# Perceiver layer on one core: the low halves of heads 8 to 15's keys are made in the second pass over the context, not in the first

## The chip, the cores and the metric

The kernel runs on one core of one Trainium2 chip. The metric is the device time of one execution in microseconds (us). Before the change it is 483.58 us, the median of 3 runs (482.57 to 485.65).

## What is computed

A perceiver layer in float32. 128 query rows of width 256 attend with 16 heads of 16 columns to a context of 12544 rows; then the 128 rows attend to each other; then a feed-forward part whose weights and activations are rounded to a few bits. The part that the change touches is the first attention:

```python
qh = (layernorm(x) @ Wq.T + bq).reshape(128, 16, 16)
kh = (ctx @ Wk.T + bk).reshape(12544, 16, 16)
vh = (ctx @ Wv.T + bv).reshape(12544, 16, 16)
scores = einsum('qhd,khd->hqk', qh, kh) / 4
scores = where(mask, -1e7, scores)
x = x + einsum('hqk,khd->qhd', softmax(scores), vh)
```

## The kernel before

**Float32 on TensorE (PE) in parts.** PE multiplies a rounded type, f32r, in one go. A float32 number is therefore split into a high part (the number rounded to f32r) and a low part (what is left). The keys are needed in both parts.

**Two passes over the context.** The context is cut into 14 blocks (NB) of 7 tiles of 128 rows, 896 keys (BK) each. The first pass finds for every query and head a maximum of the scores; the second forms the scores again, subtracts that maximum, takes exp and adds up the values. What passes from one to the other goes through DRAM.

**First pass, a block.** It has 16 slots, of which the eight even ones hold work: by `PROJECTIONS`, four are a quarter of the keys (m = 0 holds heads 0 to 7, m = 1 heads 8 to 15; n is the half of the 896 keys) and four are values of one or two tiles. For a quarter, PE does six matmuls into `ps_k` (L888), ScalarE (ACT) adds the bias and writes the rounded keys `k_hi` (L472), and VectorE (DVE) writes what is left, `k_lo` (L657). PE may not write `ps_k` again before `lo_ready` tells that DVE has read it. Values: PE L897, ACT L478. After each slot PE also forms scores of one group of heads with the bfloat16 upper halves of `k_hi` (L931). Half of these DVE reduces to a maximum (L691); ACT copies the other half as bfloat16 (L488) and DVE takes it into a running maximum (L696). Every 8 groups DVE folds the block's maxima (L702). At slot 2j the scores belong to group j + 4 of the block before (j < 4) or to group j - 4 of this block.

**The context's own split.** ACT rounds the next block's context in four pieces (L442), and GpSimd (POOL) subtracts (L379). A piece of POOL's waits for DVE's running maxima:

```python
pool.wait_ge(run_taken, (s - 2) * NG + LAG + 2 * n)
```

so the last piece (n = 3) for the next block waits for group 1 of the present one, whose scores come at slot 10. PE's next block begins with `pe.wait_ge(ctx_split, (s + 1) * PIECES)`.

**Between the passes.** PE forms the last four groups' scores; DVE folds all running maxima (L727 to L731) while PE keeps its clock up with 23 matmuls on zeros (L942); PE turns the maxima into rows (L1016), and ACT (L548) and DVE (L737) write these into `q_stack`.

**Second pass.** `k_stack` has two buffers. Of four neighbouring rows of partitions, one holds ones (it meets the row of maxima), two hold `k_hi` and one holds `k_lo`, each by a DMA of its own (SyncE, L314: six for a block, 448 KB each). PE multiplies (L1045), ACT takes exp (L559), PE adds up the values (L1058). A block has 8 units of 6 and 8 pairs of heads. The keys of block b are loaded once block b - 2 is scored, since they take its buffer. PE's code is a loop of two blocks, gone round six times, and two blocks written out behind it (L1095). DVE has only the feed-forward weights to round here (L743 to L753).

Of the kernel before, what the change touches and what calls it, by code (L numbers as in the profile page):

```python
# [4 lines left out]
H = 16  # L5
HD = 16
D = H * HD
Q = 128
# [5 lines left out]
T = 7  # L14
# [18 lines left out]
SLOTS_P = 4  # L33

# [24 lines left out]
def perceiver_layer(nc: bass.Bass, x_d, ctx_d, maskn_d, maskt_d, wqn_d, wqr_d, bqn_d, bqr_d, wk_d, bk_d, wv_d, bv_d,  # L59
# [5 lines left out]
    k_hi_d = nc.dram_tensor("k_hi_scratch", [NB, DC, P, BK], f32, kind="Internal").ap()  # L65
# [3 lines left out]
    with ExitStack() as stack_of_contexts:  # L69
# [19 lines left out]
        ctx_bufs = (ctx_t, sb("ctx_b", [P, DC * BK])[:, :])  # L89
        k_hi = sb("k_hi", [P, 2, DC, BK], f32r)  # L90
        k_upper = k_hi[:, :, :, :].bitcast(bf16).rearrange("p b m (k h) -> p b m k h", h=2)[:, :, :, :, 1]
        k_lo = sb("k_lo", [P, DC, BK], f32r)
        k_stack = sb("k_stack", [P, 2, PR, BK], f32r)

        ctx_parts = k_stack[:, 1, :, :].rearrange("p (b c l) k -> p b c l k", b=2, c=2)
# [43 lines left out]
        magic = sb("magic", [P, 3])  # L139
        self_max = sb("self_max", [P, H], bf16)  # L140
# [27 lines left out]
        stack_in = [sem(f"stack_in{i}") for i in range(2)]  # L168
# [9 lines left out]
        hi_ready, lo_ready = sem("hi_ready"), sem("lo_ready")  # L178
        max_scored, max_taken = sem("max_scored"), sem("max_taken")
# [26 lines left out]
        s_probs_t = middle[:, H * Q:2 * H * Q].rearrange("p (j n q) -> p j n q", j=4, n=4)  # L206
        w_blocks = w_raw.rearrange("p (n b) -> p n b", b=BLOCK)
# [43 lines left out]

        def scored_in(slot):
            u = slot // 2
            return (1, u + LAG) if u < LAG else (0, u - LAG)
# [4 lines left out]
        def _(sp):  # L259
# [31 lines left out]
            def store_keys(s, par, m):  # L291
                sp.wait_ge(hi_ready, (s * DC + m + 1) * 2)
                sp.dma_start(k_hi_d[s, m], k_hi[:, par, m, :].bitcast(f32)).then_inc(hi_stored[par][m], 16)
                sp.wait_ge(lo_ready, (s * DC + m + 1) * 2)
                sp.dma_start(k_lo_d[s, m], k_lo[:, m, :].bitcast(f32)).then_inc(lo_stored[m], 16)
# [5 lines left out]
            with sp.Fori(1, NB // 2) as i:  # L301
                for par in range(2):
                    s = i * 2 - 2 + par
                    load(s + 2, par)
                    store_keys(s, par, 0)
                    store_keys(s, par, 1)
                    store_values(s, par)

            def load_keys(b, par):

                for m in range(DC):
                    for slot in range(1, STRIDE):
                        src = (k_lo_d if slot == 2 else k_hi_d)[b, m]
                        sp.dma_start(k_stack[slot::STRIDE, par, m * PR // 2:(m + 1) * PR // 2, :].bitcast(f32),  # L314
                                     src.rearrange("(p r) k -> r p k", r=2 * HD)).then_inc(stack_in[par], 16)

            def load_values(b, par):
                sp.dma_start(v_in[:, par * T * H * VW:(par + 1) * T * H * VW], v_d[b]).then_inc(v_back[par], 16)
# [7 lines left out]
            load_keys(0, 0)  # L326
# [7 lines left out]
            load_values(0, 0)  # L334
            wait_keys_stored(1)
            sp.wait_ge(consts_set, 9)
            load_keys(1, 1)
            sp.wait_ge(v_stored[1], 16)
            load_values(1, 1)
            for m in range(DC):  # L340
                for par in range(2):
                    sp.wait_ge(hi_stored[par][m], 16 * NB // 2)
                sp.wait_ge(lo_stored[m], 16 * NB)
            for par in range(2):
                sp.wait_ge(v_stored[par], 16 * NB // 2)

            sp.wait_ge(lo_ready, NB * DC * 2)
# [4 lines left out]
            with sp.Fori(1, NB // 2) as i:  # L352
                for par in range(2):
# [945 lines left out]
```

## Time and profile before

| | before |
|---|---|
| median of 3 runs | 483.58 us |
| the profiled execution: device time, span | 485.21 us, 483.50 us |
| mean granted clock of TensorE | 0.979 of full |
| busy: PE, ACT, DVE, POOL | 455.1, 384.4, 275.6, 99.6 us |
| first pass, until DVE's last running maximum | to 228.7 us |
| second pass | from 235.3 to 436 us |
| second attention and feed-forward | to 483.5 us |

The span runs from the first to the last instruction. Busy times are sums over the span, and the two passes have different limits, so they are read by stretch. The granted clock is the share of full speed that TensorE was given: it has two levels, 2.4 GHz (1.00) and 1.2 GHz (0.50).

### The profile page before, as it was taken

How to read it: one execution, taken by the hardware profiler on the slowest of the kernel's cores; microseconds unless marked ns; L12 is line 12 of the kernel's file. 1: busy time of each engine (PE TensorE's matmuls, PEld its weight loads, DVE VectorE, ACT ScalarE, POOL GpSimd, SP SyncE). 2: the span in 40 equal slices, each digit the busy share in tenths (PEclk: the TensorE clock that was granted, in tenths of full speed). 3: DMA queues.
4: the chain of work that ended last, by engine and by line, in shares of the span. 5: the costliest groups of instructions: out<-in, count | busy, mean ns of one | idle time of the engine just before them, and what ended most of it. 6: DMA issues, size and time to landing. Idle time of an engine off the chain costs nothing.

```text
span 483.5 us, 15996 instructions
## 1 busy us (share of the span) xinstructions
PE 455.1 (94%) x6464; PEld 357.4 (74%) x6464; DVE 275.6 (57%) x406; ACT 384.4 (80%) x436; POOL 99.6 (21%) x101
## 2 busy tenths in 40 slices
PE   8799999999999999996899999999999999999896
PEld 4666667666676666672588999999999999985463
DVE  5579999999999999999479400000000000004566
ACT  7678888888888888875378999999999999993423
POOL 1598532343334333305000000000000000000000
PEclk9989999999999999997789999999999999999999
DMA  8986667866668766958918877777888777500000
GB/s 263 357 335 219 262 228 292 327 241 241 256 245 327 283 238 260 379 227 315 414 57 327 326 246 263 285 269 275 301 327 309 268 263 265 209 3 2 1 1 14
DMA packets 34986, 117.50 MB, mean 243 GB/s; under 512 B 4240, under 2 KB 10768, under 8 KB 34960
## 3 DMA queue, kind: packets, MB, share of 16 engines
q1 hardware_dynamic: 30784, 110.58, 60.7%
q0 software_dynamic: 4032, 6.42, 4.4%
q8 instruction: 19, 0.31, 0.3%
q10 hardware_dynamic: 144, 0.13, 0.1%
q14 instruction: 7, 0.06, 0.0%
HBM read 74.44 MB, written 39.47 MB: 236 GB/s over the span
## 4 chain that ended last, share of the span: by engine, by line
PE 46%; DVE 5%; ACT 1%; issue 1%; ACTq 0%; DVEq 0%
PE ps_a L1045 21%; PE ps_k L1058 19%; DVE early L727 1%; PE ps_a L1215 1%; PE ps_k L1232 1%; PE ps_a L942 1%; PE ps_k L1094 0%; PE ps_a L1142 0%; ACT middle L573 0%; PE ps_a L1122 0%; ACT early L559 0%; PE ps_a L1202 0%; DVE small L808 0%; PE ps_a L1194 0%; DVE early L817 0%
## 5 line engine op out<-in xcount | busy, mean ns | idle before, releaser
L691 DVE TENSOR_REDUCE block_max<-ps_a 128x2 f32<-128x896 f32 x112 | 121.2, 1084 | 0.2 <-PE ps_a L931 0.2
L1045 PEld LDWEIGHTS ps_a<-q_stack,k_stack 64*128 64x128 f32 x1568 | 98.6, 191 | 14.8 <-issue 12.7
L1045 PE MATMUL ps_a<-q_stack,k_stack 64*128 64x128 f32 x1568 | 107.9, 283 | 1.0 <-issue 0.5
L488 ACT CAST early<-ps_a 128x896 bf16<-128x896 f32 x104 | 94.7, 911 | 6.0 <-PE ps_a L931 6.0
L559 ACT ACTIVATE early<-ps_a 128x1536 f32<-128x1536 f32 (+1 forms) x56 | 90.3, 1662 | 10.4 <-PE ps_a L1045 10.4
L559 ACT ACTIVATE middle<-ps_a 128x1536 f32<-128x1536 f32 (+1 forms) x56 | 90.4, 1663 | 8.5 <-PE ps_a L1045 8.5
L759 DVE COPY early<-ps_k 128x256 f32<-128x256 f32 x2 | 0.8, 420 | 164.4 <-PE ps_k L1058 164.4
L897 PE MATMUL ps_a<-w_hi,k_stack 128*128 128x256 f32 x392 | 69.0, 298 | 0.0
L888 PE MATMUL ps_k<-k_stack,w_hi 128*128 128x448 f32 x224 | 60.8, 392 | 4.9 <-POOL k_stack L379 4.3
L696 DVE TENSOR_TENSOR early<-early 128x896 bf16<-128x896 bf16 x104 | 64.2, 618 | 0.0
L897 PEld LDWEIGHTS ps_a<-w_hi,k_stack 128*128 128x128 f32 x392 | 53.4, 190 | 11.4 <-issue 11.4
L931 PE MATMUL ps_a<-k_hi,q_pair 32*128 32x448 bf16 x448 | 43.0, 373 | 12.0 <-ACT early L488 9.4
L888 PEld LDWEIGHTS ps_k<-k_stack,w_hi 128*128 128x128 f32 x224 | 38.0, 189 | 20.0 <-issue 14.6
L1058 PE MATMUL ps_k<-middle,v_in 128*17 128x128 f32 x1568 | 49.5, 278 | 0.0
L1058 PE MATMUL ps_k<-early,v_in 128*17 128x128 f32 x1568 | 48.4, 273 | 0.1
L478 ACT COPY early<-ps_a 128x512 f32<-128x512 f32 (+1 forms) x56 | 30.3, 542 | 20.7 <-PE ps_a L897 20.7
L379 POOL TENSOR_TENSOR k_stack<-ctx_b,k_stack 128x448 fp32r<-128x448 f32 x28 | 32.2, 1154 | 55.4 <-DVE early L696 52.0
L472 ACT ACTIVATE k_hi<-ps_k,bk 128x448 fp32r<-128x448 f32 x56 | 36.1, 644 | 9.3 <-PE ps_k L888 9.3
L657 DVE SCALAR_TENSOR_TENSOR k_lo<-ps_k,bk,k_hi 128x448 fp32r<-128x448 f32 x56 | 38.1, 680 | 9.0 <-ACT k_hi L472 8.7
L1058 PEld LDWEIGHTS ps_k<-middle,v_in 128*17 128x17 f32 x1568 | 41.1, 99 | 2.6
L1058 PEld LDWEIGHTS ps_k<-early,v_in 128*17 128x17 f32 x1568 | 40.4, 97 | 2.3 <-ACT early L559 0.4
L435 POOL DMA_DIRECT2D mask_b<-in_maskt x12 | 6.3, 528 | 172.6 <-PE ps_a L1045 172.6
(188 smaller groups left out, 434.5 us busy)
## 6 DMA issues: line engine op xcount, KB each, us to landing
k_stack<-k_hi_scratch SPq DMA_DIRECT2D x56, 448.0 KB, 6.1
v_scratch<-early SPq DMA_DIRECT2D x14, 952.0 KB, 5.5
v_in<-v_scratch SPq DMA_DIRECT2D x14, 952.0 KB, 7.8
k_hi_scratch<-k_hi SPq DMA_DIRECT2D x28, 448.0 KB, 2.8
k_lo_scratch<-k_lo SPq DMA_DIRECT2D x28, 448.0 KB, 3.3
k_stack<-k_lo_scratch SPq DMA_DIRECT2D x28, 448.0 KB, 5.9
ctx_b<-in_ctx SPq DMA_DIRECT2D x7, 896.0 KB, 7.6
early<-in_ctx SPq DMA_DIRECT2D x6, 896.0 KB, 7.5
```

What stands on the lines that cost most here:

```text
L379: nc.gpsimd.tensor_tensor(ctx_lo[:, par, c, half], ctx_bufs[par][:, c * BK:(c + 1) * BK][:, half], ctx_hi[:, par, c, half].bitcast(f32), A ...
L472: nc.scalar.activation(k_hi[:, par, m, n * HK:(n + 1) * HK], ps_k[:, 0:HK], ACT.Identity, bias=bk[:, m:m + 1]).then_inc(hi_ready, 1)
L488: nc.scalar.copy(staged[:, u % 2], pair_scores(u, 0)).then_inc(max_copied, 1)
L559: nc.scalar.activation(probs[u % SLOTS_P][:, 0:width], ps_a[:, UNIT_BANK[u % 2]:UNIT_BANK[u % 2] + UP[u % 2] // 2, :].rearrange("p a n -> ...
L657: nc.vector.scalar_tensor_tensor(k_lo[:, m, half], ps_k[:, 0:HK], bk[:, m:m + 1], k_hi[:, par, m, half].bitcast(f32), ALU.add, ALU.subtrac ...
L691: nc.vector.tensor_reduce(block_max[:, 2 * u:2 * u + 2, par], pair_scores(u, 1), AX.X, ALU.max).then_inc(max_taken, 1)
L696: nc.vector.tensor_tensor(copied_rows(u), copied_rows(u), staged[:, u % 2], ALU.max).then_inc(run_taken, 1)
L888: last = nc.tensor.matmul(ps_k[:, 0:HK], w[:, 0, c, m * P:(m + 1) * P], part[:, par, c, n * HK:(n + 1) * HK], start=(k == 0), stop=(k == l ...
L897: last = nc.tensor.matmul(ps_v[:, n * D:(n + 1) * D], part[:, par, c, t * P:(t + 1) * P], w[:, 1, c, :], start=(j == 0), stop=(j == len(te ...
L931: last = nc.tensor.matmul(outs[-1], q_pair[rows, head % 2, m, :], k_upper[rows, par, m, keys], start=True, stop=not masked, skip_group_che ...
L1045: last = nc.tensor.matmul(ps_a[:, base + bank, at * Q:(at + 1) * Q], k_stack[half, b_par, a, t * P:(t + 1) * P], q_stack[half, a, ab, :], ...
L1058: last = nc.tensor.matmul(attended[32 * j:32 * j + VW, c * Q:(c + 1) * Q], v_ring[:, b_par, t, h, :], probs[slot][:, col * Q:(col + 1) * Q ...
```

## The change

For blocks 2 to 13, the keys of heads 8 to 15 (m = 1) are written by ACT unrounded, in float32, and stored once; DVE makes no `k_lo` for them and SyncE stores none (blocks 0 and 1 stay as they were; `WHOLE = 2`). All three copies in the stack are loaded from that one tensor. In the second pass DVE turns them, in the stack, into the high and low parts: for each of 4 rows (`RAW`) of a block a tensor_scalar writes a rounded, signed copy into a side buffer and a scalar_tensor_tensor adds it to the row (blocks 2 to 13, 96 instructions in all), and PE waits for that with `stack_split`. The weights' rounding is put between these.

The stack gets a third buffer. It lies where `k_hi`, `ctx_b` and `k_lo` lie in the first pass, so ACT fills it with ones between the passes, in two instructions of 128x3584, and SyncE then loads block 2 into it, ahead of the weights. From then on the keys of block b + 1 are loaded once block b - 2 is scored. The order of a block's DMAs is m = 1 first. PE's second pass is a loop of six blocks, gone round twice, and two blocks behind it.

```diff
+BUFS = 3
+WHOLE = 2
+RAW = PR // 2
...
-        k_stack = sb("k_stack", [P, 2, PR, BK], f32r)
+        stacks = sb("stacks", [P, BUFS, PR, BK], f32r)
+        k_full = third[:, 0:2 * DC * BK].rearrange("p (b m k) -> p b m k", b=2, m=DC)
...
+        def split_first(s, m):
+            return m == 0 or isinstance(s, int) and s < WHOLE
...
+                if split_first(s, m):
+                    sp.wait_ge(lo_ready, low_keys_done(s, m, 1))
+                    sp.dma_start(k_lo_d[s, m], k_lo[:, m, :]).then_inc(lo_stored[m], 16)
...
+            sp.wait_ge(third_filled, DC)
+            load_keys(2)
+
             sp.wait_ge(row_max_ready, NB + 1)
...
-            with sp.Fori(1, NB // 2) as i:
-                for par in range(2):
-                    b = i * 2 + par
+            for b in range(2, NB):
+                if b + 1 < NB:
                     sp.wait_ge(scored, (b - 1) * UNITS)
-                    load_keys(b, par)
-                    sp.wait_ge(prob_slots_free, (b - 1) * UNITS + SLOTS_P)
-                    load_values(b, par)
+                    load_keys(b + 1)
+                sp.wait_ge(prob_slots_free, (b - 1) * UNITS + SLOTS_P)
+                load_values(b)
...
+            for m in range(DC):
+                nc.scalar.activation(stacks[:, 0, m * PR // 2:(m + 1) * PR // 2, :].rearrange("p a (n k) -> p (a n) k", n=2),
+                                     zeros_b[:, 0:HK].unsqueeze(1).to_broadcast([P, PR, HK]), ACT.Identity,
+                                     bias=ones_c[:]).then_inc(third_filled, 1)
...
-                    if work[0] == "k":
+                    if work[0] == "k" and split_first(s, work[1]):
                         low_keys(s, par, work[1], work[2])
...
+            def split_stack(b):
+
+                arrived(b, 1)
+                round_row(b, 0)
+                for n in range(RAW):
+                    if n + 1 < RAW:
+                        round_row(b, n + 1)
+                    done = (b - WHOLE) * RAW + n
+                    dve.wait_ge(rounded, done + 1)
+                    row = stacks[:, (b + 1) % BUFS, PR - RAW + n, :]
+                    nc.vector.scalar_tensor_tensor(row, row.bitcast(f32), slot_is[:, 2:3], signed[done % len(signed)].bitcast(f32),
+                                                   ALU.mult, ALU.add).then_inc(stack_split, 1)
...
-                    pe.wait_ge(lo_ready, (s * DC + m) * 2 + n)
+                    if split_first(last_s, last_m):
+                        pe.wait_ge(lo_ready, low_keys_done(last_s, last_m, last_n))
+                    else:
+                        pe.wait_ge(hi_ready, (s * DC + m) * 2 + n)
...
+                def arrive(b, j):
+                    pe.wait_ge(stack_in[j % BUFS][0], (b - j) * 16 + j // BUFS * 48 + 48)
+                    pe.wait_ge(stack_split, b * RAW)
...
-                with pe.Fori(0, NB // 2 - 1) as i:
-                    two_blocks(i, False)
-                two_blocks(NB // 2 - 1, True)
+                period = 2 * BUFS
+                with pe.Fori(0, NB // period) as i:
+                    blocks(i * period, period, False)
+                blocks(NB // period * period, NB % period, True)
```

On DVE, in the first pass's loop, the slots 8 to 14 of a block (REGISTER_ALU and ISA set registers), before:

```order
L702 TENSOR_TENSOR block_max<-block_max 128x16
L654 ISA
L657 SCALAR_TENSOR_TENSOR k_lo<-ps_k,bk,k_hi 128x448
L690 ISA
L691 TENSOR_REDUCE block_max<-ps_a 128x2
L694 REGISTER_ALU
L695 REGISTER_ALU
L696 TENSOR_TENSOR early<-early 128x896
```

and the same place now (`third` holds what `k_hi` and `k_lo` held):

```order
L731 TENSOR_TENSOR block_max<-block_max 128x16
L719 ISA
L720 TENSOR_REDUCE block_max<-ps_a 128x2
L723 REGISTER_ALU
L724 REGISTER_ALU
L725 TENSOR_TENSOR early<-early 128x896
```

The scalar_tensor_tensor behind the fold is gone; the one at slot 12 too, while those at slots 0 and 4 stay.

On PE, at the end of the second pass's loop, before:

```order
L1045 MATMUL ps_a<-q_stack,k_stack 128x128 x19
L1058 MATMUL ps_k<-early,v_in 17x128 x28
L1095 REGISTER_ALU
L1095 COMPARE_AND_BRANCH
L1045 MATMUL ps_a<-q_stack,k_stack 128x128 x28
```

and now:

```order
L1122 MATMUL ps_a<-q_stack,stacks 128x128 x16
L1135 MATMUL ps_k<-early,v_in 17x128 x28
L1173 REGISTER_ALU
L1173 COMPARE_AND_BRANCH
L1122 MATMUL ps_a<-q_stack,stacks 128x128 x28
```

The work on either side of the branch is the same; between the loop's first row and this branch stand 59 rows of the program before and 180 now, three times as much code.

On DVE, in the second pass, the first block that is split in the stack, ahead of the weights' first instruction:

```order
L803 MEMSET peak 128x2
L784 TENSOR_SCALAR w_hi<-stacks,hi_sign,slot_is 128x896
L784 TENSOR_SCALAR w_lo<-stacks,hi_sign,slot_is 128x896
L797 SCALAR_TENSOR_TENSOR stacks<-stacks,slot_is,w_hi 128x896
L784 TENSOR_SCALAR early<-stacks,hi_sign,slot_is 128x896
L797 SCALAR_TENSOR_TENSOR stacks<-stacks,slot_is,w_lo 128x896
L784 TENSOR_SCALAR w_hi<-stacks,hi_sign,slot_is 128x896
L797 SCALAR_TENSOR_TENSOR stacks<-stacks,slot_is,early 128x896
L797 SCALAR_TENSOR_TENSOR stacks<-stacks,slot_is,w_hi 128x896
L806 TENSOR_REDUCE w_scale<-early 128x144
```

Eight instructions for a block, all new; four before or behind each large instruction of the weights' rounding follow for the next blocks.

## Rows read from the trace of the kernel before

**Rows 1.** Windows: us; busy us (instructions) of PE, PEld, DVE, ACT, POOL; PEclk; DMA; GB/s.

```profile
40.00:228.00 188.00, 174.26 (x1213) 125.13 (x1213) 187.70 (x266) 156.50 (x245) 71.26 (x62) 0.99 0.73 275
240.00:436.00 196.00, 195.35 (x4678) 177.34 (x4676) 26.92 (x11) 178.47 (x112) 6.33 (x12) 0.98 0.67 250
```

**Rows 2.** Timeline of DVE, one block: start, duration, what ran.

```profile
155.81 0.68 DVE L657 SCALAR_TENSOR_TENSOR k_lo<-ps_k,bk,k_hi 128x448 fp32r<-128x448 f32 x1
156.40 1.08 DVE L691 TENSOR_REDUCE block_max<-ps_a 128x2 f32<-128x896 f32 x1
...
158.93 0.61 DVE L696 TENSOR_TENSOR early<-early 128x896 bf16<-128x896 bf16 x1
...
170.59 0.68 DVE L657 SCALAR_TENSOR_TENSOR k_lo<-ps_k,bk,k_hi 128x448 fp32r<-128x448 f32 x1
```

**Rows 3.** Timeline of PE, where a block ends and the next begins.

```profile
160.21 0.38 PE L931 MATMUL ps_a<-k_hi,q_pair 32*128 32x448 bf16 x4 [0.42 <-ACT early L488]
...
160.89 1.08 PE L888 MATMUL ps_k<-k_stack,w_hi 128*128 128x448 f32 x4 [0.31 <-POOL k_stack L379]
```

**Rows 4.** Timeline of POOL, the piece that this block waits for.

```profile
159.62 1.14 POOL L379 TENSOR_TENSOR k_stack<-early,k_stack 128x448 fp32r<-128x448 f32 x1 [2.61 <-DVE early L696]
```

**Rows 5.** Waits, the whole span: total us, times, longest us.

```profile
PE ps_k L888 <- POOL k_stack L379: 4.3, 12, 0.6
```

**Rows 6.** Timeline of PE in block 1, and the start of block 2.

```profile
34.92 1.08 PE L888 MATMUL ps_k<-k_stack,w_hi 128*128 128x448 f32 x4
...
38.57 1.08 PE L888 MATMUL ps_k<-k_stack,w_hi 128*128 128x448 f32 x4
...
42.31 0.88 PE L888 MATMUL ps_k<-k_stack,w_hi 128*128 128x448 f32 x3 [0.32 <-POOL k_stack L379]
```

**Rows 7.** Timeline between the passes.

```profile
225.95 0.91 ACT L488 CAST early<-ps_a 128x896 bf16<-128x896 f32 x1 [0.67 <-PE ps_a L931]
...
228.13 0.62 DVE L696 TENSOR_TENSOR early<-early 128x896 bf16<-128x896 bf16 x1
...
233.99 0.61 PE L1016 MATMUL ps_a<-eye_b,neg_max 128*1 128x128 bf16 x16 [1.38 <-DVE neg_max L731]
234.48 1.07 ACT L548 ACTIVATE q_stack<-ps_a 1x512 fp32r<-1x512 f32 x2 [7.62 <-PE ps_a L1016]
```

**Rows 8.** Groups of instructions by shape: count, busy us, mean ns, idle before.

```profile
L559 ACT ACTIVATE middle<-ps_a 128x2048 f32<-128x2048 f32 x28 | 52.4, 1873 | 0.5 <-PE ps_a L1045 0.5
L746 DVE TENSOR_TENSOR early<-early,w_rec 128x4608 f32<-128x4608 f32 x1 | 5.0, 4959 | 0.0
L747 DVE TENSOR_SCALAR early<-early 128x4608 f32<-128x4608 f32 x1 | 2.6, 2559 | 0.0
```

**Rows 9.** Timeline of SyncE: first load of the keys of two blocks in a row.

```profile
280.45 0.61 SPq L314 DMA_DIRECT2D k_stack<-k_hi_scratch  x1
...
294.33 0.63 SPq L314 DMA_DIRECT2D k_stack<-k_hi_scratch  x1
```

**Rows 10.** Timeline of PE in the loop's first round in the second pass.

```profile
262.11 0.89 PE L1045 MATMUL ps_a<-q_stack,k_stack 64*128 64x128 f32 x13 [0.55 <-issue]
```

**Rows 11.** DMA queues, windows 240 to 268.5, 258 to 262, 268.5 to 413 (all of its queues).

```profile
q8 instruction: 5, 0.08, 1.2%
...
q8 instruction: 1, 0.02, 1.5%
...
q1 hardware_dynamic: 10685, 39.22, 72.1%
q0 software_dynamic: 1584, 2.52, 5.7%
```

**Rows 12.** DMA issues by line: count, KB each, median us from issue to landing.

```profile
v_in<-v_scratch SPq DMA_DIRECT2D x14, 952.0 KB, 7.8
out<-x ACTq DMA_DIRECT2D x1, 128.0 KB, 1.8
```

**Rows 13.** A window of 2 us at the start of the second pass.

```profile
238.00:240.00 2.00, 2.00 (x9) 0.71 (x7) 0.00 (x0) 1.74 (x2) 0.00 (x0) 0.50 1.01 422
```

More of the change, by code:

```diff
@@ L206, in perceiver_layer @@
         s_probs_t = middle[:, H * Q:2 * H * Q].rearrange("p (j n q) -> p j n q", j=4, n=4)
+        signed = [w[:, :, :, :].rearrange("p a c n -> p (a c n)")[:, 0:BK] for w in (w_hi, w_lo)]
+        signed.append(early[:, WN + 4096:WN + 4096 + BK].bitcast(f32r))
         w_blocks = w_raw.rearrange("p (n b) -> p n b", b=BLOCK)
@@ L299, in store_values, with move, load_keys, load_values @@
                 sp.dma_start(v_d[s], v_new[:, par].rearrange("p t h w -> p (t h w)")).then_inc(v_stored[par], 16)
-            with sp.Fori(1, NB // 2) as i:
-                for par in range(2):
[L303 to L311, printed above, removed]
-                    for slot in range(1, STRIDE):
[L313 to L318, printed above, removed]
+            def move(s, par):
+                load(s + 2, par)
+                store_keys(s, par, 0)
+                store_keys(s, par, 1)
+                store_values(s, par)
+            for s in range(WHOLE):
+                move(s, s)
+            with sp.Fori(WHOLE // 2, NB // 2 - 1) as i:
+                for par in range(2):
+                    move(i * 2 + par, par)
+            def load_keys(b):
+                for m in (1, 0):
+                    for slot in range(1, STRIDE):
+                        src = (k_lo_d if slot == 2 and split_first(b, m) else k_d)[b, m]
+                        sp.dma_start(stacks[slot::STRIDE, (b + 1) % BUFS, m * PR // 2:(m + 1) * PR // 2, :].bitcast(f32),
+                                     src.rearrange("(p r) k -> r p k", r=2 * HD)).then_inc(stack_in[b % BUFS][m], 16)
+            def load_values(b):
+                sp.dma_start(v_in[:, b % 2 * T * H * VW:(b % 2 + 1) * T * H * VW], v_d[b]).then_inc(v_back[b % 2], 16)
             def wait_keys_stored(b):
@@ L471, in evacuate_keys @@
                     act.wait_ge(hi_stored[par][m], (s - par) * 8)
-                nc.scalar.activation(k_hi[:, par, m, n * HK:(n + 1) * HK], ps_k[:, 0:HK], ACT.Identity,
+                keys = k_full[:, par, m, n * HK:(n + 1) * HK]
+                nc.scalar.activation(keys.bitcast(f32r) if first or m == 0 else keys, ps_k[:, 0:HK], ACT.Identity,
                                      bias=bk[:, m:m + 1]).then_inc(hi_ready, 1)
@@ L753, in _ @@
             nc.vector.transpose(w_raw[:, DC * F:2 * DC * F], w_raw[:, 0:DC * F]).then_inc(weights_ready, 1)
+            for b in range(7, NB):
+                split_stack(b)
             dve.wait_ge(bv_in, 16)
@@ L1073, in two_blocks, with blocks @@
+                def blocks(first, count, final):
+                    for u in range(0, count * UNITS, 2):
+                        ending = final and u == count * UNITS - 2
                         for w in (u, u + 1):
                             if not ending:
-                                pe.wait_ge(exp_done, i * (2 * UNITS) + w + 1)
-                                nxt = (w + 2) % (2 * UNITS)
-                                if nxt == 0:
-                                    arrive(i * 2 + 2, 0)
```

123 lines of the change are left out of this document (76 added, 47 removed).

## The prediction

> **What bounds the kernel now.** I read the windows of the two passes first, since one average over the span hides two limits. In the first pass DVE works 187.7 of 188 us while PE works 174.3; in the second PE works 195.4 of 196 and DVE 26.9 [rows 1]. So the first pass looks bound by DVE, the second is bound by PE, and the change takes work from DVE in the first and gives it more in the second. The question is what stands right behind DVE in the first pass, and whether the second pass stays as it is for PE.
>
> The timeline of DVE gives the period of a block: the scalar_tensor_tensor at slot 8 starts at 155.81 and again at 170.59, so 14.78 us [rows 2]. For PE, where a block ends and the next begins, two waits stand in a row: the last scores wait 0.42 us for ACT's copy of the scores before (`ps_a` L931 <- `early` L488), and the next block's first keys wait 0.31 us for POOL's piece of the context [rows 3]. All else on PE follows without a gap that the timeline names. How fast PE goes by itself is to be seen in block 1, where DVE has no running maxima to take and isn't full: from one quarter of the keys to the next 3.65 us (34.92 to 38.57), and 3.74 from the last quarter to block 2 (38.57 to 42.31), with 0.32 of it a wait for POOL [rows 6]. Without that wait a block is 3 x 3.65 + 3.42 = 14.37 us for PE. So PE stands only 0.41 us behind DVE.
>
> **First pass: what is removed.** Two scalar_tensor_tensor in each of blocks 2 to 13, 24 in all. Each holds DVE for 0.59 us (155.81 to the next start at 156.40) [rows 2], 14.2 us in all. Of these PE can pass on only what it waited for. The chain behind the removed one at slot 8 is: DVE's running maximum at 158.93, done at 159.54 [rows 2]; POOL's piece from 159.62 to 160.76 [rows 4]; PE's keys at 160.89 [rows 3]. With the 0.59 gone, POOL's piece ends 0.59 earlier and PE could begin at 160.30. But its last scores, held by ACT and not by DVE, start at 160.21 and take some 0.30 us to issue, so PE begins at 160.51: it gains 0.38 here, with 0.21 us to spare on POOL. The wait for ACT stays, since it is a loop of PE and ACT alone (keys done, ACT's bias, ACT's copy), and 0.42 us of every block stays lost. Counted over the span, the waits for POOL are 12 with 4.3 us together [rows 5]; the first of them, 0.32 us, falls at the start of block 2, before anything is removed [rows 6], so 4.0 us is the least that goes. By the periods it is 14.78 - 14.37 = 0.41 for each of the 11 block starts from 3 to 13, 4.5 us. I take 4.5, since this holds the small waits that no row names.
>
> DVE then needs 14.78 - 2 x 0.59 = 13.60 us for a block of 14.37: it is no longer full, and it comes to the end of the pass with less behind it. Now its last maximum ends at 228.75, 1.89 us after ACT's last copy at 226.86 [rows 7]. A maximum can't end before the copy and its own 0.62 us, 0.74 with a release of 0.12; I take 0.9 as left, so 1.0 us is gained; between 0.5 and 1.15. Together **5.5 us off the first pass**, between 4.5 and 5.7. The stores that go (12 of 448 KB) free DMA that nothing waits for. PE's wait on `ps_k` now ends with ACT instead of DVE, but it is not among its waits at this place, so nothing more comes of it.
>
> **Between the passes: ACT's fills.** The nearest row is exp on 128x2048, 1.87 us [rows 8]; by length 3584 elements are 3.28 us, two are 6.6 us, with a start-up counted too often in it. ACT was idle there for 7.62 us, from 226.86 to 234.48 [rows 7]. By the 1.0 us that DVE gains beyond ACT, this idle time shrinks to 6.6. So the fills fit exactly: I take nothing, with 0.5 us for either side. Before the change, the idle time of an engine hid it; that cover is now used up. SyncE issues block 2's keys after the fills and the weights after them, so the weights come later, but they are wanted only at the end of the span.
>
> **Second pass: DVE's split.** A block has 4 tensor_scalar and 4 scalar_tensor_tensor of 128x896. From the two shapes of 4608 elements, 2.56 us and 4.96 us [rows 8], these are 0.50 and 0.96 us, so 5.9 us for a block; if both went at the dearer rate, 7.7. A block lasts 13.88 us (280.45 to 294.33) [rows 9], and the keys of a block are loaded two blocks ahead. Even with one of the weights' instructions (4.96) ahead of it and 8 us of load, 5.0 + 8 + 7.7 = 20.7 us is less than 27.8. Its price is nothing. For the whole pass DVE has some 71 + 27 of 196 us to do.
>
> **Second pass: PE's code.** This is the part that the change doesn't speak of. In the loop's first round PE stops once for 0.55 us with nothing that it waits for but "issue" [rows 10]. The DMA queues tell what goes on: the instruction queue q8 moves 5 packets of 16 KB between 240 and 268.5 us, as PE goes through the two blocks' code for the first time, and one of them falls into 258 to 262, when the data queue is full; between 268.5 and 413 us, in the further rounds, only q1 and q0 move anything [rows 11]. So code is fetched as PE comes to it, five packets for two blocks, and what has been fetched for a two-block loop is kept. A loop of six blocks is 15 packets. Two costs follow.
>
> The first is at each burst of data. Before, one burst (that of 252 to 265) met fresh code under full pace, and it cost 0.55. Now fresh code runs at least through six blocks, and through all 14 if a 15-packet loop isn't kept; 11 bursts (keys of blocks 3 to 13) lie in it. Between 0 and 0.55 each, that is 0 to 6.05 us; I take half, 3.0, less the 0.55 that is paid now: **2.5 us**. Half, since of the packets fetched in the loop's first round only one was late.
>
> The second is the return. No row shows a jump to code that isn't there. It costs between nothing (it is there) and the landing of one DMA, 1.8 us on an idle queue to 7.8 on a full one [rows 12]. I take **1.9**, since a packet is small and the return comes once.
>
> As for the Trainium skill, "Runtime: NRT & Kernel Launch", section "Instruction fetch mechanics", says that PE's instruction memory has 128 KiB, 2048 instructions, is filled in 16 KiB blocks in sequence, and that a taken branch to a page not in its window stalls for a fetch. By that rule the two-block loop (80 KB) is kept, as the trace agrees, and the six-block loop (some 240 KB) isn't, so the return would stall once and the second round be fetched again; by its remark that crossing a block is "mostly hidden" the first cost would be near zero.
>
> **The sum.** On the profiled execution: 485.21 - 5.5 + 2.5 + 1.9 = 484.1. It is 1.63 us above the median of 483.58, to which the same steps give 483.58 - 1.1 = **482.5 us**. About 1%, 4.8 us, is what a measurement of this kernel can tell from no change.
>
> **The rivals.**
> 1. *The code costs nothing* (the loop is kept, or the fetches stay ahead). For it: five rounds of a two-block loop without any gap, and four packets of the first round without one. Against it: the one gap under full data queues. It gives 483.58 - 5.5 = 478.1. Chance 0.24.
> 2. *The clock.* At 238 to 240 us PE is granted 0.50 of its clock, 1.2 GHz [rows 13], after it had idled for 1.38 us before L1016 and again behind it [rows 7]. The keep-clock matmuls now end nearer to DVE's result, so the dip could shrink. A mean clock of 0.979 over 483.5 us (the table) means 20 us at half pace; I take 8 of them to lie here, which cost 4 us. It gives 483.58 - 1.1 - 4 = 478.5, or 474 with rival 1. Chance 0.06.
> 3. *The first pass keeps its stall.* The spare of 0.21 us on POOL's piece is small; if DVE's maxima start later by 0.3 to 0.6, PE waits on for POOL, and only 1 to 3 us are saved instead of 5.5. Or ACT's fills come late by 1 or 2 us. It gives 484.5 to 486.5. Chance 0.14.
> 4. *Slower: PE starves for code.* The same mechanism as in the forecast, at its upper end. Place: each burst after the first round's start, and the return. Price: 11 x 0.55 - 0.55 = 5.5, and at the return two packets one after the other at 3.9 to 7.8 on a full queue: up to 13.3 in all, so 483.58 - 5.5 + 13.3 = 491.4. From 5.5 on it eats the gain, from 10.3 the kernel is slower by over 1%. For it: the gap that there is came at such a burst. Against it: packets are 16 KB beside transfers of 448 KB. Chance 0.09.
> 5. *It doesn't take the work away.* Excluded by the order of DVE's instructions, in which the two are gone from each loop's block.
>
> The forecast (480.5 to 485) has 0.45, and 0.02 is for what I don't see.
>
> **How the numbers follow.** Range: from 477.0, a little below rival 1, to 487.5, above rival 3. It leaves out rival 4's upper part (0.09) and the faster half of rival 2 with the unseen (0.05). Faster by over 1% (under 478.7): rivals 1 and half of 2, 0.27. Slower by over 1% (over 488.4): 0.10. Within 1%: 0.63.
>
> **What would show it.** Right: the starts of PE's block in the first pass 14.37 apart, no wait for POOL L379 there but for block 2, the 0.42 for ACT still there, DVE with idle time at last; the pass ends 5.5 us earlier. ACT's first row into `q_stack` with no or little idle time. In the second pass PE's gaps named "issue": up to one for each burst, the longest at the return after six blocks (about 83 us behind the pass's start), and q8 packets all along it, some 36 in place of 10. Wrong: a PE wait for `stack_split` or the stack's DMAs; gaps none or far longer than 0.55; a first pass that goes at 13.6 us a block, which would mean that PE's own 14.37 holds hidden waits for DVE.

## The result, and the profile after

| | before | after |
|---|---|---|
| median (lowest to highest) | 483.07 us (478.08 to 485.65), 4 runs | 495.55 us (492.54 to 499.45), 4 runs |
| profiled execution: device time, span | 485.21, 483.50 us | 492.54, 490.8 us |
| mean granted clock | 0.979 | 0.986 |

The ratio is 1.030, with a 95% interval of 1.017 to 1.042: the changed kernel is slower by 3%, where 482.5 us and no difference over 1% had been forecast. It lies outside the range given, 477.0 to 487.5. Ratios, here and below, leave out the executions of a slower state (485.65 us here; 486.39, 816.66 and 519.72 us in the experiments), medians and ranges don't, and the profiled execution of before, 485.21 us, is of that state too.

The page of the changed kernel: PE's and the others' busy time, the chain that ended last, and PE's two groups of the second pass (busy us, mean ns | idle before, and its releaser).

```profile
PE 455.2 (93%) x6464; PEld 356.6 (73%) x6464; DVE 347.8 (71%) x482; ACT 390.5 (80%) x438; POOL 100.9 (21%) x101
...
PE 71%; ACT 9%; issue 8%; DVE 7%; SPq 2%; DMA 1%; ACTq 0%; POOL 0%; DVEq 0%; POOLq 0%
...
L1122 PE MATMUL ps_a<-q_stack,stacks 64*128 64x128 f32 x1568 | 107.7, 281 | 10.1 <-issue 9.2
```

PE's busy time is what it was (455.1 before); "issue", time in which PE waits for nothing that the profile shows, is 8% of the chain. The same windows as in [rows 1], moved to where the passes now lie:

```profile
40.00:222.00 182.00, 171.60 (x1197) 123.62 (x1196) 174.19 (x240) 154.97 (x242) 69.43 (x60) 0.99 0.66 250
...
240.00:445.00 205.00, 191.41 (x4502) 171.91 (x4503) 107.83 (x106) 172.43 (x108) 7.18 (x12) 0.98 0.61 230
```

In the first pass DVE is no longer full (174.2 of 182 us; it was 187.7 of 188). In the second, PE is idle for 13.6 of 205 us, where it had 0.65 of 196.

**The first pass** is shorter, as forecast. PE's block starts (the first keys of a quarter, L964), with the last scores ahead of one:

```profile
39.41 1.08 PE L964 MATMUL ps_k<-stacks,w_hi 128*128 128x448 f32 x4 [0.33 <-POOL stacks L397]
...
141.34 1.08 PE L964 MATMUL ps_k<-stacks,w_hi 128*128 128x448 f32 x4
...
155.43 0.38 PE L1007 MATMUL ps_a<-third,q_pair 32*128 32x448 bf16 x4 [0.42 <-ACT early L507]
156.07 1.08 PE L964 MATMUL ps_k<-stacks,w_hi 128*128 128x448 f32 x4 [0.26 <-issue]
...
170.46 1.08 PE L964 MATMUL ps_k<-stacks,w_hi 128*128 128x448 f32 x4
```

The wait for POOL is left at block 2 alone, and the 0.42 us for ACT stays. From 156.07 to 170.46 a block takes 14.39 us, but from 141.34 to 156.07 it takes 14.73: where the loop of two blocks goes back, 0.26 us of "issue" shows, where before had the 0.31 us for POOL [rows 3]. The waits of the whole span have 5 of these, 1.2 us.

**Between the passes**, ACT's two fills, and its first row of maxima behind them:

```profile
220.76 6.46 ACT L570 ACTIVATE stacks<-zeros_b,ones_c 128x3584 fp32r<-128x3584 bf16 x2
227.74 1.07 ACT L577 ACTIVATE q_stack<-ps_a 1x512 fp32r<-1x512 f32 x2 [0.53 <-PE ps_a L1093]
```

ACT is idle for 0.53 us where it had been for 7.62 [rows 7], and it still waits for PE: the fills held nobody up. From block 2's start to this row before took 192.17 us (42.31 to 234.48) and now takes 188.33: a gain of 3.84 us. That the row comes 6.74 us earlier has a second cause ahead of block 2, which starts at 39.41 instead of 42.31. There the profiled execution of before had the granted clock at half for some 3 us (0.63 over the window 24 to 28.6 us), which the one of after hadn't. That is no part of the change: it is luck of the two executions.

**The second pass: DVE.** Its timeline over the first block that it splits:

```profile
236.78 0.75 DVE L784 TENSOR_SCALAR w_hi<-stacks,hi_sign,slot_is 128x896 fp32r<-128x896 f32 x1 [6.74 <-DMA stacks<-k_scratch]
...
238.10 1.15 DVE L797 SCALAR_TENSOR_TENSOR stacks<-stacks,slot_is,w_hi 128x896 fp32r<-128x896 f32 x1
...
242.60 1.14 DVE L797 SCALAR_TENSOR_TENSOR stacks<-stacks,slot_is,w_hi 128x896 fp32r<-128x896 f32 x1
```

Eight instructions, from 236.78 to 243.74: 7.0 us for a block. Who waits for them is in the waits of the second pass (total us, times, longest):

```profile
PEld ps_a L1122 <- issue: 22.0, 58, 6.3
...
PE ps_a L1122 <- issue: 9.2, 4, 6.0
PEld ps_k L1135 <- issue: 5.1, 6, 1.5
PE ps_k L1135 <- issue: 3.6, 6, 1.3
...
PEld ps_a L1122 <- DVE stacks L797: 0.2, 1, 0.2
```

One weight load waits 0.2 us for DVE, and PE nowhere waits for the stack's DMAs.

**The second pass: PE's code.** These are PE's stops in it that are named "issue", ten in all, from its timeline:

```profile
246.08 1.05 PE L1135 MATMUL ps_k<-early,v_in 128*17 128x128 f32 x27 [0.69 <-issue]
...
253.39 1.00 PE L1122 MATMUL ps_a<-q_stack,stacks 64*128 64x128 f32 x14 [1.77 <-issue]
...
269.66 1.06 PE L1135 MATMUL ps_k<-early,v_in 128*17 128x128 f32 x29 [0.44 <-issue]
...
281.58 1.06 PE L1135 MATMUL ps_k<-middle,v_in 128*17 128x128 f32 x31 [1.30 <-issue]
...
313.73 1.27 PE L1135 MATMUL ps_k<-early,v_in 128*17 128x128 f32 x35 [0.30 <-issue]
...
327.91 3.25 PE L1122 MATMUL ps_a<-q_stack,stacks 64*128 64x128 f32 x28 [5.98 <-issue]
331.09 3.04 PE L1135 MATMUL ps_k<-middle,v_in 128*17 128x128 f32 x56
...
365.22 1.06 PE L1135 MATMUL ps_k<-early,v_in 128*17 128x128 f32 x29 [0.54 <-issue]
...
382.18 1.22 PE L1122 MATMUL ps_a<-q_stack,stacks 64*128 64x128 f32 x17 [1.14 <-issue]
...
393.00 1.33 PE L1122 MATMUL ps_a<-q_stack,stacks 64*128 64x128 f32 x19 [0.32 <-issue]
...
409.25 1.27 PE L1135 MATMUL ps_k<-early,v_in 128*17 128x128 f32 x35 [0.29 <-issue]
```

Nine of them are in the midst of straight code, 6.79 us together. The tenth, at 327.91, is the loop's return behind six blocks: 5.98 us. The sum is 12.77 us, where before had 0.55 [rows 10]. The instruction queue moved 38 packets between 240 and 445 us, where it had moved 10 between 240 and 436; between 330 and 409 us, the loop's second round, alone:

```profile
q8 instruction: 14, 0.23, 1.1%
```

So the second round is fetched again; in [rows 11] the further rounds of the two-block loop had fetched nothing. And the return costs more than its stop. The window of the stop, and one behind it:

```profile
322.00:327.90 5.90, 0.00 (x0) 0.00 (x0) 3.07 (x5) 0.52 (x1) 0.00 (x0) 0.93 1.02 378
328.00:334.00 6.00, 6.00 (x84) 5.15 (x84) 3.79 (x4) 3.33 (x2) 0.00 (x0) 0.51 0.20 80
```

While PE stood, the DMA engines were full (the column behind the clock); behind the stop the clock is 0.51, that is 1.2 GHz. The 28 and 56 matmuls at 327.91 and 331.09 take 3.25 and 3.04 us, and 1.82 and 1.72 at full clock (rows of e1 below): 2.8 us more.

### The profile page after: what moved, and what is told of

Same layout as the page of the kernel before. It is cut to its first block, busy times and chain, and to the rows that moved or that the text cites. A ratio compares the mean times of both kernels' runs of the same rounds, so it can differ in the third digit from the quotient of the medians.

```text
span 490.8 us, 15866 instructions
## 1 busy us (share of the span) xinstructions
PE 455.2 (93%) x6464; PEld 356.6 (73%) x6464; DVE 347.8 (71%) x482; ACT 390.5 (80%) x438; POOL 100.9 (21%) x101
## 4 chain that ended last, share of the span: by engine, by line
PE 71%; ACT 9%; issue 8%; DVE 7%; SPq 2%; DMA 1%; ACTq 0%; POOL 0%; DVEq 0%; POOLq 0%
PE ps_a L1122 20%; PE ps_k L1135 19%; PE ps_a L973 11%; PE ps_k L964 10%; PE ps_a L1007 5%; ACT early L507 4%; DVE block_max L720 2%; PE ps_k L1018 2%; DVE early L725 1%; ACT stacks L460 1%; DMA third<-in_ctx 1%; ACT middle L588 1%; ACT third L491 1%; PE ps_a L1293 1%; PE ps_k L1310 1%
## 5 line engine op out<-in xcount | busy, mean ns | idle before, releaser
L1122 PE MATMUL ps_a<-q_stack,stacks 64*128 64x128 f32 x1568 | 107.7, 281 | 10.1 <-issue 9.2
L1122 PEld LDWEIGHTS ps_a<-q_stack,stacks 64*128 64x128 f32 x1568 | 98.0, 189 | 24.1 <-issue 22.0
L973 PE MATMUL ps_a<-w_hi,stacks 128*128 128x256 f32 x392 | 68.5, 297 | 0.0
L964 PE MATMUL ps_k<-stacks,w_hi 128*128 128x448 f32 x224 | 60.7, 391 | 2.2 <-issue 1.2
L973 PEld LDWEIGHTS ps_a<-w_hi,stacks 128*128 128x128 f32 x392 | 53.1, 188 | 11.3 <-issue 11.2
L1007 PE MATMUL ps_a<-third,q_pair 32*128 32x448 bf16 x448 | 42.5, 369 | 10.3 <-ACT early L507 8.6
L964 PEld LDWEIGHTS ps_k<-stacks,w_hi 128*128 128x128 f32 x224 | 37.8, 188 | 16.6 <-issue 12.9
L397 POOL TENSOR_TENSOR stacks<-third,stacks 128x448 fp32r<-128x448 f32 x28 | 32.2, 1154 | 53.0 <-DVE early L725 51.0
L491 ACT ACTIVATE third<-ps_k,bk 128x448 fp32r<-128x448 f32 (+1 forms) x56 | 36.1, 644 | 5.4 <-PE ps_k L964 5.2
L973 PE MATMUL ps_a<-w_lo,stacks 128*128 128x256 f32 x196 | 38.8, 280 | 0.0
```

The source lines that it names most:

```text
L397: nc.gpsimd.tensor_tensor(ctx_lo[:, par, c, half], ctx_bufs[par][:, c * BK:(c + 1) * BK][:, half], ctx_hi[:, par, c, half].bitcast(f32), A ...
L491: nc.scalar.activation(keys.bitcast(f32r) if first or m == 0 else keys, ps_k[:, 0:HK], ACT.Identity, bias=bk[:, m:m + 1]).then_inc(hi_read ...
L964: last = nc.tensor.matmul(ps_k[:, 0:HK], w[:, 0, c, m * P:(m + 1) * P], part[:, par, c, n * HK:(n + 1) * HK], start=(k == 0), stop=(k == l ...
L973: last = nc.tensor.matmul(ps_v[:, n * D:(n + 1) * D], part[:, par, c, t * P:(t + 1) * P], w[:, 1, c, :], start=(j == 0), stop=(j == len(te ...
L1007: last = nc.tensor.matmul(outs[-1], q_pair[rows, head % 2, m, :], k_upper[rows, par, m, keys], start=True, stop=not masked, skip_group_che ...
L1122: last = nc.tensor.matmul(ps_a[:, base + bank, at * Q:(at + 1) * Q], stacks[half, (b + 1) % BUFS, a, t * P:(t + 1) * P], q_stack[half, a, ...
```

## The experiments

The theory: PE's code in a loop longer than what is kept costs the time, and nothing else in the change does. The rivals: DVE's splitting or the third buffer's traffic slows PE; or the first pass gained less than it seems to. Comparisons with before are made on the same chip; its median was 481.65 us for e1 to e4 and 482.16 for e5 to e8 (13 runs each).

**e1: before, with only PE's second pass as a loop of six blocks.** Nothing else is changed.

```diff
+LOOP = 6
...
-                with pe.Fori(0, NB // 2 - 1) as i:
-                    two_blocks(i, False)
-                two_blocks(NB // 2 - 1, True)
+                with pe.Fori(0, NB // LOOP) as i:
+                    blocks(i * LOOP, LOOP, False)
+                blocks(NB // LOOP * LOOP, NB % LOOP, True)
```

> The kernel before with PE's second pass written as a loop of six blocks, gone round twice, and two blocks behind it, in place of two blocks gone round six times; nothing else. Theory A (PE starves for code): the second pass shows the gaps of the changed kernel, some 12 to 13 us with about 6 of it at the loop's return, some 28 more packets on the instruction queue, and a clock dip behind the return (some 3 us): 483 + 15 = 498 us, at least 493. Theory B (DVE's split in the stack, or its traffic, slows PE or ACT): this kernel has none of that work, so 483 us, unchanged.

505.29 us (501.81 to 507.85), ratio 1.050 [1.043, 1.056]. PE stops for "issue" 17 times in the second pass, 14.7 us together. (One more stop, 1.73 us at 291.40, is put down to ACT, but PE's weight load at the same place waits 1.64 us for "issue", so it may be an eighteenth.) The return and what follows it in PE's timeline:

```profile
332.12 3.25 PE L1046 MATMUL ps_a<-q_stack,k_stack 64*128 64x128 f32 x28 [5.70 <-issue]
335.30 3.16 PE L1059 MATMUL ps_k<-middle,v_in 128*17 128x128 f32 x56
338.39 1.82 PE L1046 MATMUL ps_a<-q_stack,k_stack 64*128 64x128 f32 x28
340.14 1.72 PE L1059 MATMUL ps_k<-early,v_in 128*17 128x128 f32 x56
```

The code alone costs 23.6 us, 7 more than the 498 us expected and more than the whole change does, which has the first pass's gain to set against it. Neither DVE's new work nor the third buffer is needed for the loss.

**e2: before, with all 14 blocks of PE's second pass written out.** No return, but fresh code all along.

```diff
-                with pe.Fori(0, NB // 2 - 1) as i:
-                    two_blocks(i, False)
-                two_blocks(NB // 2 - 1, True)
+                blocks(0, NB, True)
```

> The kernel before with all 14 blocks of PE's second pass written out, no loop. Theory A: the stall at the return and the clock dip behind it are gone, the small gaps at code that comes for the first time stay, for 14 blocks: 6 to 7 us, so 489 to 490 us, ten to nine below the six-block loop. If the whole cost hung on the return, 483; if all on fetches, like the six-block loop. Theory B: 483.

487.64 us (486.2 to 491.61), ratio 1.010 [1.004, 1.016]. Three stops:

```profile
277.35 0.61 PE L1058 MATMUL ps_k<-early,v_in 128*17 128x128 f32 x11 [1.85 <-issue]
...
324.08 1.55 PE L1045 MATMUL ps_a<-q_stack,k_stack 64*128 64x128 f32 x24 [0.86 <-issue]
...
394.70 0.63 PE L1058 MATMUL ps_k<-early,v_in 128*17 128x128 f32 x15 [0.39 <-issue]
```

Fresh code costs 3.1 us of stops, against 14.7 in e1, though as much of it is fetched (45 packets in the span, 47 in e1). So straight code is fetched mostly in time, and it is the loop that makes the large loss. But 3.1 us isn't the whole price: the median is 6.0 us above before's. In the profiled execution, the slowest of the four, the second pass takes 210.0 us (232.59 to 442.62), 13.0 more than e4's below, and the clock is at half at its start and also behind two of these stops:

```profile
234.00:245.00 11.00, 11.00 (x120) 8.45 (x120) 2.12 (x1) 6.66 (x4) 0.00 (x0) 0.54 0.70 291
277.50:286.00 8.50, 8.50 (x123) 7.24 (x115) 0.00 (x0) 3.95 (x3) 0.53 (x1) 0.60 0.44 138
325.00:330.00 5.00, 5.00 (x89) 4.30 (x88) 0.00 (x0) 3.25 (x3) 0.53 (x1) 0.66 0.55 179
```

**e3: after, with all 14 blocks written out.** The same edit in the changed kernel.

```diff
-                period = 2 * BUFS
-                with pe.Fori(0, NB // period) as i:
-                    blocks(i * period, period, False)
-                blocks(NB // period * period, NB % period, True)
+                blocks(0, NB, True)
```

> The changed kernel with all 14 blocks of PE's second pass written out, no loop. Theory A: 6.0 us of stall at the return and 3.4 us of half clock behind it go, 6.8 us of small gaps stay: 495.5 - 9.4 = 486 us. Theory B: unchanged, 492 to 499.

480.26 us (478.96 to 484.21, 10 runs), ratio to before 0.999 [0.995, 1.002]: 15.3 us less than after's median, by PE's code alone (before's own medians beside the two differ by 1.4 us). Seven stops, 3.59 us. From ACT's first row to DVE's copy of the sums its second pass is 203.9 us (227.54 to 431.43), after's is 215.9. Of these 12.0 us, 9.2 are the stops that go (12.77 - 3.59) and 2.8 the half clock behind the return: nothing is left over between these two. The time is some 6 us under the 486 expected, since the stops in straight code fell as well, from 6.8 to 3.6 us.

**e4: before, without the low halves of heads 8 to 15 in blocks 2 to 13.** It leaves them out altogether: DVE makes none, none are stored, and in the stack the high half lies in their place. The blocks' loads come in after's order, m = 1 first.

```diff
+        def split_first(s, m):
+            return m == 0 or isinstance(s, int) and s < WHOLE
...
-                        src = (k_lo_d if slot == 2 else k_hi_d)[b, m]
+                        src = (k_lo_d if slot == 2 and split_first(b, m) else k_hi_d)[b, m]
...
-                    if work[0] == "k":
+                    if work[0] == "k" and split_first(s, work[1]):
```

> The kernel before with the first pass's part alone: for blocks 2 to 13 DVE makes and SyncE stores no low half of the keys of heads 8 to 15; their high half is loaded in its place (so these heads' scores are left without the low part). Second pass, buffers and loop as before. If the first pass's gain is what the changed kernel's trace shows, its end comes 6 to 7 us earlier, and if the clock dip at the second pass's start goes with PE's shorter wait there, some 3 us more: 473 to 477 us. By my prediction's sum 477.6. If the gain in the changed kernel came from the new buffers or stores and not from DVE's work, less than that.

474.31 us (473.35 to 477.2), ratio 0.986 [0.980, 0.992]. PE has no stop for "issue" in the second pass, which takes 197.0 us (227.43 to 424.46). The first pass has after's two periods, 14.4 and 14.7. This is the gain of the first pass by itself, together with what the clock at the second pass's start makes of it (rival 2, below).

**e5: the whole change, but with two stack buffers and PE's loop of two blocks.** The third buffer, its fills and the early load of block 2 go; keys are loaded two blocks ahead again; the split in the stack stays.

```diff
-        stacks = sb("stacks", [P, BUFS, PR, BK], f32r)
+        k_stack = sb("k_stack", [P, 2, PR, BK], f32r)
...
-            sp.wait_ge(third_filled, DC)
-            load_keys(2)
```

> The changed kernel's idea without its third buffer: for blocks 2 to 13 the keys of heads 8 to 15 are unsplit in the first pass and split by DVE in the stack, but the stack has two buffers as before and PE's second pass is the loop of two blocks, whose code is kept; no fills by ACT. From the changed kernel's trace a block's split holds DVE 6.9 us (4 x 0.66 + 4 x 1.06). The keys of m = 1 land some 5 to 7 us after block b - 2 is scored, so a block's split is ready 12 to 14 us behind that, and PE wants it at 1.65 + 13.84 = 15.5. If that holds, the gain of the first pass stays and nothing is paid: 474 to 477 us. If the landing comes a few us later (values and weights are in the same queue), PE waits for stack_split 1 to 3 us a block, 12 to 36 us in all: 486 to 510 us.

475.82 us (474.72 to 476.84), ratio 0.989 [0.982, 0.997]: it computes the same as before and after and beats both. Its second pass takes 197.0 us, as e4's does without any split, so DVE's 12 x 7 us cost nothing. The window of its second pass:

```profile
240.00:427.00 187.00, 186.75 (x4556) 171.18 (x4548) 110.21 (x108) 174.00 (x110) 6.33 (x12) 1.00 0.68 255
```

DVE works 110.2 us beside PE, which is idle for 0.25 of 187 us. The DMA engines are as busy as ever (0.68), so their load doesn't slow PE either; what it can slow is the fetch of code (e7), of which there are 10 packets here.

**e6: before, with a loop of four blocks.** As e1 with `LOOP = 4`: three rounds, two returns.

> The kernel before with PE's second pass as a loop of four blocks, gone round three times, and two blocks: code of some 10 to 11 packets, against 5 that are kept and 16 that aren't. If 8 packets (128 KB) are kept, it is fetched anew in each round and returns twice: 2 x (5.8 + 3.4 for the clock behind it) and some 5 us of small gaps: 500 to 508 us, 45 packets or so on the instruction queue. If four blocks are kept: 484 to 486 us and 25 packets.

515.41 us (511.52 to 519.72), ratio 1.069 [1.056, 1.083]. Eleven stops, 19.5 us, of which the two returns are

```profile
307.01 3.25 PE L1046 MATMUL ps_a<-q_stack,k_stack 64*128 64x128 f32 x28 [6.98 <-issue]
...
375.77 3.25 PE L1046 MATMUL ps_a<-q_stack,k_stack 64*128 64x128 f32 x28 [6.26 <-issue]
```

So a loop of four blocks isn't kept while one of two (5 packets) is: its first round moves 10 packets and each of the two others 13 (windows 237 to 300, 300 to 369.5, 369.5 to 432). Each return is paid in full, again with the clock at half behind it (28 matmuls in 3.25 us). The time lies above the 500 to 508 us expected: the second pass is 30.7 us longer than e4's, of which the stops are 19.5. Of the rest, the clock has a part, behind the returns and once more behind the stop of 1.16 us that ends at 430.11 (0.65 over 430.1 to 435).

**e7: e1 without the loads of keys and values for blocks 2 to 13.** It leaves them out; the scores and sums of these blocks are formed from blocks 0 and 1 again.

```diff
-            with sp.Fori(1, NB // 2) as i:
-                for par in range(2):
-                    b = i * 2 + par
-                    sp.wait_ge(scored, (b - 1) * UNITS)
-                    load_keys(b, par)
-                    sp.wait_ge(prob_slots_free, (b - 1) * UNITS + SLOTS_P)
-                    load_values(b, par)
```

> The six-block loop in the kernel before, with no keys or values loaded for blocks 2 to 13 (their scores and sums are formed with blocks 0 and 1 again): the instruction queue has the DMA engines nearly to itself. If the gaps come from fetches held up behind the data's bursts, the small ones go and the return costs what a small DMA takes, 1.8 to 2.5 us in place of 5.7 to 6: 486 us. If code alone is the limit, the gaps stay at 14 us in all: 500 us.

486.71 us, from two runs (483.61 and 489.81); the ratio's interval, 0.999 to 1.025, doesn't tell it from before, and against e1's median it is 18.6 us less. PE stops once, at the return:

```profile
326.93 2.78 PE L1039 MATMUL ps_a<-q_stack,k_stack 64*128 64x128 f32 x28 [3.07 <-issue]
```

As many packets of code are fetched as in e1 (39 in the second pass), and 16 of 17 stops are gone. So, in these two executions, the stops in straight code come from the data transfers beside the fetch, and 2.6 us of the return's 5.7 too. The rest of it, 3.07 us, is there on idle DMA engines: the instruction queue moves one packet in the stop, which took 1.2 us (2.4% of 16 engines' 3.07 us), and the remainder has no row. Under load it moved two packets in each return's stop (after, e1 and both in e6). Windows of e7 in the stop and behind it:

```profile
324.00:327.00 3.00, 0.07 (x2) 0.08 (x2) 0.00 (x0) 0.57 (x1) 0.00 (x0) 1.00 0.02 5
330.00:338.00 8.00, 8.00 (x128) 6.60 (x120) 0.00 (x0) 4.95 (x3) 0.00 (x0) 0.51 0.01 2
```

The clock is granted in full during the stop and at half behind it, as in after, and again 28 matmuls at 1.2 GHz take 2.8 to 3.25 us.

**e8: before, with only slot 8's low half left out.** One DVE instruction a block instead of two; what is stored and loaded in its place is stale.

```diff
+        def split_first(s, m, n):
+            return (m, n) != (1, 0) or isinstance(s, int) and s < 2
```

> Of the first pass's part, the half of it: for blocks 2 to 13 DVE skips only the low part of heads 8 to 15's first 448 keys (slot 8 of a block; what is stored and loaded for them is left from before), and keeps the other. DVE then needs 14.78 - 0.59 = 14.19 us a block, below PE's 14.37. If PE stands right behind DVE, as the prediction has it, the period is the same as without both (14.4 to 14.7 by turns) and only the tail is a little later: 475 to 477 us. If PE gains from each removed instruction, half of the gain is lost: 478 us.

476.24 us (474.35 to 480.52, 10 runs), ratio 0.990 [0.986, 0.995]. PE's periods are e4's, 14.4 and 14.7. In the periods one instruction frees PE as far as two do: the second only gives DVE room. It shows at the pass's end: from block 13's start to ACT's first row it is 28.75 us here (201.03 to 229.78) and 27.96 in e4 (199.47 to 227.43).

## Why the prediction was wrong

Set out by its steps, in the two profiled executions, whose spans differ by 7.3 us where a difference of -1.1 was forecast. (The medians differ by 12.5: before's profiled execution is 2.1 us above its median, and after's, its fastest, 3.0 below.)

| step | forecast | measured |
|---|---|---|
| first pass, from block 2 on, with its end | -5.5 us | -3.84 |
| half clock ahead of block 2, in the run of before only | none | -2.9 |
| ACT's fills; DVE's split | 0 | 0 |
| stops in straight code, less 0.55 | +2.5 | +6.2 |
| the return's stop | +1.9 | +6.0 |
| half clock behind the return | not in the sum | +2.8 |
| half clock at the second pass's start, in the run of before only | 0 | -4.3 |
| what is in no listed stop | 0 | +3.3 |

The two parts of the second pass that are no stops come from e4, whose second pass has neither a stop for code nor a dip and takes 197.0 us: before's 201.8 less 0.55 is 4.3 above it, and after's 215.9 less 12.8 and 2.8 is 3.3 above it. The first is the clock's only by this difference; the dip itself is in the rows (0.57 over 236 to 248 us).

**The step that failed is "Second pass: PE's code".** Its mechanism was right: code is fetched as PE comes to it, two blocks are kept, six aren't, each fetch under a burst of data can be late, and the return stalls once. All of this is in the traces, and e1 shows that it makes the loss by itself, e3 that without the loop it goes. Wrong were both terms' sizes. The stops in straight code were put at half of 0.55 us for each of 11 bursts; there were nine of 0.29 to 1.77 us. The single gap of before was taken as the upper end of such gaps, and one value bounds nothing from above. The return was put at 1.9 us, near the landing of one DMA on an idle queue; it is 5.98, nearer the upper bound of 7.8 that the same step gave. The place should have told that. SyncE issues a block's loads once a block is scored, and the return stands behind the first two units of the next block, so it falls into the burst: at all four returns with loads the DMA engines are full during the stop (0.99 to 1.02 in after, e1 and e6). After's SyncE timeline shows it ahead of the return, where PE stops at 321.9:

```profile
316.78 2.56 SPq L337 DMA_DIRECT2D stacks<-k_scratch  x4
...
321.99 0.33 SPq L341 DMA_DIRECT2D v_in<-v_scratch  x1
```

The order of the code and of the loads was to be had before the run. And e7 shows 3.07 us even on idle engines, so the lower rows had no ground. The third cost, the clock, was in no term, although [rows 13] and [rows 7] show just this, a stop of PE and 0.50 behind it. So what happened is rival 4, given 0.09, and more than it: its 13.3 us compare with 12.2 of stops and 2.8 of clock, and its 491.4 us with 495.55. Its two packets at the return are in the traces (e7 above); its size for each burst (0.55) is not.

The Trainium skill, "Runtime: NRT & Kernel Launch", section "Instruction fetch mechanics", says that a taken branch out of the window that is held stalls for a fetch. The traces agree for loops of four and six blocks (5.98, 5.70, 6.98 and 6.26 us under load, 3.07 without). But the window it states is two pages of 16 KiB, and by that the loop of two blocks, 5 packets, would stall too, which it doesn't [rows 11]. The prediction took the 128 KiB as the window; the runs show only that the limit lies between 5 and 10 packets. Its remark that crossing a block of code is "mostly hidden" holds in e7, without loads, nearly so in e2 and e3 (3.1 and 3.6 us), and not in after (6.8 us) or e1 (9.0).

**First pass: right in kind, 1.7 us too large.** The period of 14.37 was measured as 14.39 for every second block. At the loop's returns it is 0.3 more, with the new 0.26 of "issue". So from block 2's start to block 13's the gain is 2.95 us (163.07 before, 160.12 after), where 4.5 were forecast; behind it 0.9 of the 1.0. When a wait goes, what is late next was to be named, and this wasn't. That it is the branch's cost, hidden under POOL's wait before, is likely but not shown: the second pass's loop of two blocks has no such stop at its returns (e4, e5). e8 confirms that PE stands right behind DVE, so rival 3 didn't happen.

**Fills and split: right.** The fills took 6.46 us against 6.6, and fitted. The split took 7.0 us a block against 5.9, within the bound of 7.7, and e5 shows that it costs nothing.

**Rival 2, the clock, is not settled.** The dip at the start of the second pass is in two of the ten profiled executions, before's (0.57 over 236 to 248 us) and e2's (0.54 over 234 to 245). It isn't in after, e3, e4, e5 and e8, but not in e1, e6 and e7 either, whose first pass is before's. What goes with it is the idle time that the rival named: ahead of the maxima's turn into rows (L1016 before) PE waits 1.38 and 1.52 us for DVE in those two, and between nothing and 0.87 us in the other eight. No experiment changes that wait alone, and over the five executions with before's first pass it goes from 0.20 to 1.52 us by itself. Before's runs beside e1 to e4 go from 478.6 to 484.8 us at mean clocks of 0.993 to 0.979. The medians of e4 and e5 are 7.3 and 6.3 us below before's, more than the 3.84 us of the first pass. Whether the change makes the dip rarer or these runs were lucky, no run here tells.

**What stays open.** 3.3 us of after's second pass are in no stop of PE's list, as many of e3's, and 6.2 of e1's. Some of it is stops too short to be listed: PE's weight loads wait 27.1 us for "issue" in after's second pass and 12.5 in e4's, 14.6 more, which is 1.8 above the 12.8 listed. In e1 and e3 it is alike (31.7 and 17.9 us: 4.5 and 1.8 above their lists). About 1.5 us remain without a name in after and e3, and 1.7 in e1, where it can be the stop of 1.73 us put down to ACT. Both the number and the length of the stops come from one profiled execution of each kernel. After's median is 3.0 us above its profiled execution, at mean clocks down to 0.975; which stops or dips make that isn't seen.

## What to carry to other kernels

Before a loop is lengthened, for instance so that its body divides by a new number of buffers, count its code in the instruction queue's packets. Here 5 packets a round are kept and 10 are not; then each return stops PE for 6 to 7 us while data moves, the clock is at half behind it, and the straight code has stops too (4.5 and 2.3 us in after's two rounds). If a body must be longer than that, write it out in full (e3), though that cost 6.0 us against the kept loop in e2; or choose a number of buffers that divides the short one (e5, the best version here that computes the whole, 475.8 us). A cost that a trace shows once, under luckier conditions, is an example and no upper bound; price it at the place where it will stand.

## What the runs showed of the hardware

- A return to code that isn't held costs 3.07 us with idle DMA engines, of which the packet itself took 1.2 us, and 5.7 to 7.0 us with full ones, when two packets are moved in the stop. I had not expected so long a stop on idle engines.
- Behind each of the five such returns (after, e1, e7 and two in e6), the granted clock is at half: 28 matmuls that take 1.82 us take 2.8 to 3.25. Over the stop itself it is 1.00 in e7 and 0.76 to 0.95 in the others, so there it falls before the stop ends.
- Shorter stops had it behind them in some cases only: e2's of 1.85 and 0.86 us and e6's of 1.16 us did, after's of 1.77 and 1.30 us didn't (1.00 over the 6 us behind each).
- Written-out code of 14 blocks has fewer stops (3.1 and 3.6 us, e2 and e3) than two rounds of six blocks (12.8 and 14.7), although as many packets are fetched; a first round of after has 4.5 us of small stops, its second 2.3. Why straight code stops less often than the loop's first round isn't settled. Nor does a burst of data explain each stop: during after's 1.14 us at 382.18 the DMA engines are idle (0.00), though they had been at 0.66 in the 3 us before.
